# Last tiles that end with the last row, blank rows at fixed addresses, and outputs of the early tiles sent later

## What is computed

```python
h = layernorm(x) * (1 + ca) + sa
x = x + ga * attention(h)                      # per row
h = layernorm(x) * (1 + cb) + sb
gates = softmax((h @ w_red) @ wg_n.T);  idx = argmax(gates)      # one expert for each row
y = gelu(h @ w1[idx] + b1[idx]) @ w2[idx] + b2[idx]
x = x + gb * y * gates[idx]
```

## Time and profile before

| | |
|---|---|
| median of 3 runs | 321.43 us (321.24 to 325.39) |
| the profiled execution | 321.42 us |
| its span, first to last instruction | 319.7 us |
| mean granted TensorE clock | 0.949 of 2.4 GHz |
| busy: PE, DVE, ACT, POOL | 86%, 74%, 70%, 49% |

### The profile page before, as it was taken

One profiled execution on the slowest core, in us unless ns is written; L12 is line 12 of the kernel. 1 busy time (PEld: TensorE's weight loads), 2 busy tenths in 40 slices (PEclk: granted clock), 3 DMA queues, 4 the chain that ended last, 5 costly groups with the idle time before them and its releaser, 6 DMA issues. The chain is left out here.

```text
span 319.7 us, 11500 instructions
## 1 busy us (share of the span) xinstructions
PE 275.4 (86%) x4012; PEld 222.2 (70%) x4013; DVE 236.5 (74%) x769; ACT 224.2 (70%) x510; POOL 158.0 (49%) x173
## 2 busy tenths in 40 slices
PE   8789799999999999999999977684949699999960
PEld 3555577777777677687677756574849599999950
DVE  2767969989979989899899999595523456666740
ACT  1377788999889799889898689364237276676730
POOL 7104144362684774755746804557743434455550
PEclk9999999999999999999999999898578899999995
DMA  5996000000010011010100205134954424444400
GB/s 148 322 333 181 0 3 4 2 2 4 4 51 27 28 51 51 29 51 28 50 28 29 76 27 152 49 102 126 243 148 121 109 67 126 119 124 108 125 22 0
DMA packets 16240, 26.16 MB, mean 82 GB/s; under 512 B 2607, under 2 KB 11059, under 8 KB 16192
## 3 DMA queue, kind: packets, MB, share of 16 engines
q1 hardware_dynamic: 12464, 16.50, 18.8%
q0 software_dynamic: 3296, 8.41, 7.7%
q10 hardware_dynamic: 432, 0.59, 0.6%
HBM read 15.32 MB, written 10.64 MB: 81 GB/s over the span
## 5 line engine op out<-in xcount | busy, mean ns | idle before, releaser
L1129 DVE SCALAR_TENSOR_TENSOR phi<-ps,ebuf 128x512 f32<-128x512 f32 x128 | 82.0, 682 | 17.9 <-ACT ebuf L540 17.4
L536 ACT ACTIVATE ebuf<-ps 128x1024 f32<-128x1024 f32 x64 | 65.6, 1026 | 16.4 <-PE ps L766 15.6
L540 ACT ACTIVATE ebuf<-ebuf 128x512 f32<-128x512 f32 x128 | 74.4, 636 | 0.1
L764 PE MATMUL ps<-hT_hi,mix_lo 128*128 128x512 f32 x128 | 58.4, 456 | 8.2 <-DVE phi L1129 4.9
L594 ACT ACTIVATE gT<-ps,b_cols 128x128 f32<-128x128 f32 x156 | 44.7, 368 | 19.8 <-issue 13.6
L866 PE MATMUL ps<-w_sb,gT 128*128 x312 | 45.9, 294 | 13.2 <-DVE y L1446 11.3
L866 PEld LDWEIGHTS ps<-w_sb,gT 128*128 128x128 f32 x312 | 41.2, 206 | 15.2 <-issue 15.2
L766 PE MATMUL ps<-hT_hi,mix_hi 128*128 128x512 f32 x128 | 50.6, 396 | 0.0
L765 PE MATMUL ps<-hT_lo,mix_hi 128*128 128x512 f32 x128 | 50.6, 395 | 0.0
L495 POOL DMA_INDIRECT out<-yo,tok x27 | 27.4, 1014 | 29.7 <-issue 15.9
L446 POOL DMA_INDIRECT sorted_rows<-rec,pos x32 | 33.0, 1030 | 8.8 <-issue 5.4
(11 more groups left out here) (197 smaller groups left out, 452.5 us busy)
## 6 DMA issues: line engine op xcount, KB each, us to landing
rin<-sorted_rows SPq DMA_DIRECT2D x39, 192.5 KB
w1b<-in_L_ffn_w SPq DMA_DIRECT2D x1, 2048.0 KB, 14.2
sorted_rows<-pad_rec SPq DMA_DIRECT2D x6, 192.5 KB
sorted_rows<-pad_rec ACTq DMA_DIRECT2D x3, 192.5 KB
w1b<-in_L_ffn_b SPq DMA_DIRECT2D x1, 512.0 KB, 6.0
sorted_rows<-rec,pos POOLq DMA_INDIRECT x32
out<-yo,tok POOLq DMA_INDIRECT x27
wmod_sb<-in_L_wmod SPq DMA_DIRECT2D x1, 384.0 KB, 3.5
```

The lines of the kernel that those rows point to most:

```text
L536: nc.scalar.activation(ebuf[:, h % 2, :, :], x_ps[h % 2], ACT.Relu, scale=-1.0).then_inc(s_neg, 1)
L540: nc.scalar.activation(ebuf[:, h % 2, j, :], ebuf[:, h % 2, j, :], ACT.Exp, scale=-1.0).then_inc(s_exp, 1)
L764: mm(x_ps[h % 2][:, j, :], mix_lo[:, j, h, :], hi, start=True, stop=False)
L1129: v.scalar_tensor_tensor(out=phi[:, h % 4, j, :], in0=x_ps[h % 2][:, j, :], scalar=0.0, in1=ebuf[:, h % 2, j, :], op0=ALU.max, op1=ALU.add ...
```

## The change

The blank rows move from behind the last row of each expert to the head of its region: every region's first 128 rows are blank records, written by SP near the start of the program (nine writes, one of them the former `DUMMY`), and the records begin 128 rows further down (`region0` starts at 128). The last tile of an expert is taken as the 128 rows that end with the expert's last row. It overlaps the tile before it (or the blank head where the expert has few rows); the rows that were in the tile before get T added to their number, and are so not written twice. Slots behind the last tile get the last tile again, with all rows turned blank. For that the table has a second hop, a limit and a mask `blank`. The eight `pad_region` writes and `carry_i` go. On POOL, the 12 early outputs are no longer sent in one go: numbers 0 to 5 go out each when the slot six later is finished, numbers 6 to 11 after slots 15, 19, 23, 27, 31 and 35; POOL's loop over the late outputs is written out.

```diff
 sp.wait_ge(c_dve, 1)
-sp.dma_start(sorted_rows[DUMMY:DUMMY + P, :], pad_rec[:, :]).then_inc(s_tail, 16)
+for e in range(E + 1):
+    sp.dma_start(sorted_rows[e * REGION:e * REGION + P, :], pad_rec[:, :]).then_inc(s_tail, 16)
...
-for s in range(RING, RING + RING // 2):
+for s in range(RING, EARLY):
     reload_slot(s, s % RING)
 sp.wait_ge(s_table, 1)
-for e in range(PADS_SP):
-    pad_region(sp, e)
-for s in range(RING + RING // 2, EARLY):
-    reload_slot(s, s % RING)
-sp.wait_ge(s_table, 2)
...
-g_.iota(region0[:, :], [[REGION, E]], base=0, ...)
+g_.iota(region0[:, :], [[REGION, E]], base=P, ...)
+g_.iota(slot_next[:, :], [[1, LATE]], base=1, ...)
+g_.iota(row_no[:, :], [[0, 1]], base=0, channel_multiplier=1, ...)
+g_.memset(last_row[:, E:E + 1], float(DUMMY))
...
-def put_early(s):
-    wait_then(f_yd, s + 1)
+def put_early(s, behind=0):
+    wait_then(f_yd, s + 1 + behind)
...
-for s in range(EARLY):
-    put_early(s)
-with pool.Fori(EARLY, WHOLE - RING + 1, RING) as s:
-    for b in range(RING):
-        put(s + b, b)
-for s in range(WHOLE, SLOTS):
+for s in range(RING):
+    put_early(s, RING)
+for s in range(EARLY, SLOTS):
     put(s, s % RING)
+    if s % 4 == 3 and s // 4 - 3 < EARLY - RING:
+        put_early(s // 4 - 3 + RING)
...
 gelu(5, 1)
-act.wait_ge(s_table, 1)
-for e in range(PADS_SP, E):
-    pad_region(act, e)
...
-    v.tensor_copy(at, rin[:, b, 3 * D:R])
+    if early:
+        v.tensor_copy(at, rin[:, b, 3 * D:R])
+    else:
+        v.scalar_tensor_tensor(out=at, in0=blank[:, bass.ds(s - EARLY, 1)], scalar=float(T), in1=rin[:, b, 3 * D:R],
+                               op0=ALU.mult, op1=ALU.add)
...
-v.tensor_copy(carry_i[:, :], carry[:, :]).then_inc(s_table, 1)
...
+v.tensor_scalar(last_row[:, 0:E], carry[:, :], -float(P), None, ALU.add).then_inc(s_last, 1)
...
+v.tensor_scalar(limit[:, :], last_row[:, 0:1], row_no[:, :], None, ALU.add)
...
+v.tensor_tensor(skip[:, 1, :], last_row[:, 1:E + 1], last_row[:, 0:E], ALU.subtract).then_inc(s_tab, 1)
...
-v.tensor_tensor(hop[:, :, :], past[:, :, :], skip[:, :]..., ALU.mult).then_inc(s_tab, 1)
+for i in range(2):
+    last = v.tensor_tensor(hop[:, i, :, :], past[:, :, :], skip[:, i, :]..., ALU.mult)
...
-v.tensor_reduce(rowf[:, 0, :], hop[:, :, :], AX.X, ALU.add).then_inc(s_tab, 1)
+v.tensor_reduce(rowf[:, :, :], hop[:, :, :, :], AX.X, ALU.add).then_inc(s_tab, 1)
...
-v.tensor_scalar(row_i[:, EARLY:SLOTS], rowf[:, 1, :], float(DUMMY), None, ALU.min).then_inc(s_table, 1)
+v.scalar_tensor_tensor(out=row_i[:, EARLY:SLOTS], in0=rowf[:, 1, :], scalar=last_row[:, 0:1], in1=raw[:, :],
+                       op0=ALU.add, op1=ALU.min).then_inc(s_table, 1)
...
+v.scalar_tensor_tensor(out=blank[:, :], in0=rowf[:, 1, :], scalar=limit[:, :], in1=raw[:, :],
+                       op0=ALU.add, op1=ALU.is_lt).then_inc(s_blank, 1)
```

More of the change, by code:

```diff
@@ L50, in adaln_kernel @@
     RECS = 3
-    PADS_SP = E - 3
     RING = 6
@@ L190, in adaln_kernel @@
         lden = sb("lden", [P, TG, E])
-        skip = sb("skip", [P, E])
+        skip = sb("skip", [P, 2, E])
+        last_row = sb("last_row", [P, E + 1])
+        limit = sb("limit", [P, 1])
+        row_no = sb("row_no", [P, 1])
+        blank = sb("blank", [P, LATE])
         past = sb("past", [P, LATE, E])
-        hop = sb("hop", [P, LATE, E])
+        hop = sb("hop", [P, 2, LATE, E])
         expf = sb("expf", [P, LATE])
         rowf = sb("rowf", [P, 2, LATE])
+        raw = sb("raw", [P, LATE])
         region0 = sb("region0", [P, E])
@@ L198, in adaln_kernel @@
         slot_no = sb("slot_no", [P, SLOTS])
+        slot_next = sb("slot_next", [P, LATE])
         exp_i = sb("exp_i", [P, SLOTS], I32)
         row_i = sb("row_i", [P, SLOTS], I32)
-        carry_i = sb("carry_i", [P, E], I32)
         rin = sb("rin", [P, RING, R])
@@ L680, in _ @@
             gelu(EARLY - 1, (EARLY - 1) % 2)
-            act.wait_ge(s_table, 3)
+            act.wait_ge(s_table, 2)
             keep_in(EARLY, EARLY)
@@ L1295, in early_past @@
                 dve.wait_ge(s_ta, 6)
-                v.tensor_tensor(hop[:, 0:EARLY, :], past[:, 0:EARLY, :], skip[:, :].unsqueeze(1).broadcast_to([P, EARLY, E]), ALU.mult)
+                v.tensor_tensor(hop[:, 0, 0:EARLY, :], past[:, 0:EARLY, :], skip[:, 0, :].unsqueeze(1).broadcast_to([P, EARLY, E]), ALU.mult)
                 v.tensor_reduce(expf[:, 0:EARLY], past[:, 0:EARLY, :], AX.X, ALU.add).then_inc(s_ta, 1)
                 dve.wait_ge(s_ta, 7)
-                v.tensor_reduce(rowf[:, 0, 0:EARLY], hop[:, 0:EARLY, :], AX.X, ALU.add).then_inc(s_ta, 1)
+                v.tensor_reduce(rowf[:, 0, 0:EARLY], hop[:, 0, 0:EARLY, :], AX.X, ALU.add).then_inc(s_ta, 1)
             def early_table():
                 dve.wait_ge(s_ta, 8)
-                v.scalar_tensor_tensor(out=row_i[:, 0:EARLY], in0=slot_no[:, 0:EARLY], scalar=float(P), in1=rowf[:, 0, 0:EARLY],
+                v.scalar_tensor_tensor(out=row_i[:, 0:EARLY], in0=slot_next[:, 0:EARLY], scalar=float(P), in1=rowf[:, 0, 0:EARLY],
                                        op0=ALU.mult, op1=ALU.add).then_inc(s_early, 1)
@@ L1313, in early_rest @@
                 v.tensor_tensor(hop_a[:, :], done[:, 1:E + 1], done[:, 0:E], ALU.subtract).then_inc(s_ta, 1)
-                v.tensor_scalar(row_base[:, :], slot_no[:, 0:LATE], done[:, 0:1], float(P), ALU.add, ALU.mult)
+                v.tensor_scalar(row_base[:, :], slot_next[:, :], done[:, 0:1], float(P), ALU.add, ALU.mult)
                 dve.wait_ge(s_ta, 11)
@@ L1507, in _ @@
             v.tensor_tensor(upto[:, :, :], tri[:, :, :], rest[:, :].unsqueeze(1).broadcast_to([P, E, E]), ALU.mult)
-            v.scalar_tensor_tensor(out=skip[:, :], in0=rest[:, :], scalar=-float(P), in1=hop_a[:, :],
-                                   op0=ALU.mult, op1=ALU.add).then_inc(s_tab, 1)
+            v.scalar_tensor_tensor(out=skip[:, 0, :], in0=rest[:, :], scalar=-float(P), in1=hop_a[:, :],
+                                   op0=ALU.mult, op1=ALU.add)
+            v.tensor_tensor(skip[:, 1, :], last_row[:, 1:E + 1], last_row[:, 0:E], ALU.subtract).then_inc(s_tab, 1)
             dve.wait_ge(s_tab, 5)
@@ L1515, in _ @@
             dve.wait_ge(s_tab, 7)
[L1516 removed]
+            for i in range(2):
+                last = v.tensor_tensor(hop[:, i, :, :], past[:, :, :], skip[:, i, :].unsqueeze(1).broadcast_to([P, LATE, E]), ALU.mult)
+            last.then_inc(s_tab, 1)
             dve.wait_ge(s_tab, 8)
[L1518 removed]
+            v.tensor_reduce(rowf[:, :, :], hop[:, :, :, :], AX.X, ALU.add).then_inc(s_tab, 1)
             dve.wait_ge(s_tab, 9)
[L1520 removed]
+            v.tensor_tensor(raw[:, :], rowf[:, 0, :], row_base[:, :], ALU.add).then_inc(s_tab, 1)
             dve.wait_ge(s_tab, 10)
[L1522 removed]
+            v.scalar_tensor_tensor(out=row_i[:, EARLY:SLOTS], in0=rowf[:, 1, :], scalar=last_row[:, 0:1], in1=raw[:, :],
+                                   op0=ALU.add, op1=ALU.min).then_inc(s_table, 1)
             v.tensor_reduce(expf[:, :], past[:, :, :], AX.X, ALU.add).then_inc(s_tab, 1)
@@ L1533, in _ @@
                 finish(s, s % RING)
+            dve.wait_ge(s_blank, 1)
             def run(s, b):
```

16 lines of the change are left out of this document (8 added, 8 removed).

## The result

The changed kernel takes 326.24 us in the median of 19 runs (324.73 to 329.59), the kernel before 322.99 us in 19 runs beside it (321.01 to 325.39): a ratio of 1.0115, 95% interval [1.009, 1.014]. Every ratio in this document is formed from the executions in the faster of two states alone, while the medians are of all, so that it can be off the quotient of the medians by up to 0.7%. It was forecast at 316.2 us (313.3 to 321.3), and it is slower.

A forecast was written before the change was run, and what follows sets the result against it. PE was taken to bound the late slots, and a stall on three engines slots 5 to 8. 321.4 - 5.6 + 0.1 + 0.1 + 0.4 = 316.4 us, with the clock's luck 316.2; range 313.3 to 321.3.

The forecast's parts named there:

- Removed: the stall: Slots 5 to 8: the wait of DVE, ACT and SP goes, 5.6 us won (5.1 to 6.2), longer table included.
- the lucky-clock rival: After 232 us: all lower-clock spells of PE go, 6.2 us won and 1.5 to 2 more, about 314; chance 0.21.
- Table: DVE's early table ahead of `add_bias(4)`: gets 1.1 us longer (0.8 to 1.6).
- Added at the start: Eight more blank writes from SP from 24.34 us on, and POOL setup: zero, at most 0.5; 0.1 in the sum.
- Moved: the early outputs: Late stretch: six more POOL writes of 1.0 us fit into its idle time; cost 0.1 us.
- Changed in the late slots: DVE's row-number copy becomes an operation with the mask: 0.4 us taken, bounds 0 and 2.7.
- The stall moves into the late slots: Three POOL outputs in a row after slots 15, 19, 23, 27, 31, 35 stall there: 329 us; chance 0.07.
- The price of one place: Each of the six late places with three outputs costs 1.3 to 3 us, taken as 2.2.
- double buffering: Late slots: absorbs 5 of the 13 us that the six places would cost.
- The outputs were not it: Early stall comes from POOL's records of group 7 and stays, if shorter: 319 to 322.5, say 321; chance 0.15.
- DVE becomes the bound: Late slots: DVE's mask operation costs 0.1 us per slot, 318.5; inside the forecast's range, no chance of its own.

The follow-up runs named there:

- without the late six: Changed kernel with early outputs 6 to 11 taken out of POOL's late loop, their rows left out of the output: 314.26 us, ratio 0.9747 to the kernel before.
- the new order alone: Kernel before, blank rows and table as they were, with only POOL's new order of outputs: 331.24 us, ratio 1.0189.
- The run to nowhere: Changed kernel with all row numbers of the six late early outputs out of bounds, so POOL works but nothing is written: 327.42 us, ratio 1.0113.
- the version with other milestones: Changed kernel, all twelve early outputs ahead of slot 12's, spread by waits on finished slots 5, 5, 6, 7, 8, 9, 10, 10, then four later points: 319.18 us.
- the run with the old order: Changed kernel with its 12 early outputs in one go behind the records of group 7, blank rows as changed: 321.26 us, ratio 0.9964.
- the last version: Changed kernel, twelve early outputs ahead of slot 12's, a 128x784 POOL memset behind writes except where DVE copies weights or ends the table: 317.19 us, ratio 0.9816.

## Why the prediction was wrong

*Removed: the stall.* Right in kind and too small. The forecast was 5.6 won with the table's 1.1 inside; without the late six the early span shrinks by 6.8 (34.75 to 27.96), which is the value of the lucky-clock rival (6.2 and up): the granted clock was 0.97 over 232 to 242 us, though 0.70 over 245 to 248. I gave the stall to blank writes and outputs together, and that holds for the sum: of the 6.8 us, moving the blank rows alone gave 0.6 (with the table's 1.0 inside), the new order alone 3.5, and only both give all. What I had not seen is that they act in two ways. The outputs hold up news; late blank rows alone make PE wait for slot 9's tile. *Table:* slot 4 took 5.73 us for 4.75, 0.98 for the 1.1 forecast.

*Added at the start.* Zero, as put: `add_bias(0)` at 206.79 for 207.37.

*Moved: the early outputs.* This is the step that failed: "In the late stretch POOL is busy 20.42 of 42 us; six more at 1.0 fit. ... Zero, with a margin of only 0.12; I take 0.1." They do fit: POOL is busy 21.37 of 42 after, and the last output follows the last `add_bias` by 1.82 us as before (1.81). But the sum priced POOL's time and not that of the engines whose news the writes hold up. That measured 12.0 us in time (326.24 against 314.26), 10.9 in the late span, for a forecast of 0.1. The Trainium skill's rule (SBUF — State Buffer, the warning that DVE can hold up a DMA issued from GpSimd) let me weigh the wrong direction: it is about what DVE does to POOL's write, here 0.3 us at most, and nothing in it covers PE's news.

*Changed in the late slots.* Forecast 0.4, measured nothing: the late span without the six is 51.22 with the mask, 51.60 without.

*The rivals.* "The stall moves into the late slots" had 0.07, and is what happened: places and mechanism as written, and a size of 13 less 5 against 10.9 measured. Its 329 does not follow from that size: 316.4 and 8 are 324.4, with all 13 it is 329.4, and 326.24 was measured. So the chance of 0.07 for more than 327.9 stood on a wrong sum. The price of one place was right (2.2; slots 17 to 33 lost 1.8 to 2.3 each, the sixth place about 1); double buffering, for which I took off 5, absorbed next to nothing at the first five: ACT waits for its transpose from the same moment as DVE for its sums, and PE needs both. My reasons against it were bytes (64 KB for 192) and the DMA share (0.44). The run to nowhere shows that bytes play no part, and the share even fell, to 0.38. The row for it was in the earlier trace rows, a "remote" wait of 1.27 us with four records in a row and nothing else. I had written that POOL's back-to-back writes alone do some of the stall, and then did not let that into the sum. "The outputs were not it" is refuted: with the records alone there was no stall at slots 5 to 8. "DVE becomes the bound" is refuted by the 51.22.

## What stays open

What is shown is that POOL's own work on indirect writes that follow each other 1.3 us apart holds up the news, whatever they move, and that between writes 1.8 us and more apart it was never seen. What exactly starts a hold is not shown. Two writes can be enough: in the changed kernel two records start at 199.54 and 200.92, and ACT takes the transpose that PE finished at 200.22 only at 202.39, "remote"; every version has this place. A news item crossed four records unharmed at 229.14 in the changed kernel; in the version with other milestones ACT had PE's transpose at 236.01, 0.04 us after its end, with two close writes before it and a third just begun (233.39 to 236.96). Yet at 261.08 two close writes on top of the steady stream were enough. A backlog that builds up would fit some of these and not all. Runs of two in the late slots, with the stream's own pace kept, were not tried. Nor is it known which part on the way from PE to DVE and ACT is held. It can't be that way alone, since SP's own instructions slow down too (the last section).

## What to carry to other kernels

Count a POOL indirect write not by its 1 us of a half-idle engine but by who waits for other engines' news while writes follow closely: look at the distance of their starts, and keep them apart (here 1.8 us). A queue that already runs at its steady pace has no free slots, even at half its busy time; what is put into it is caught up later, close together. And where several engines wait for PE, "remote" or long after its end, and go on within 0.2 us of each other, look for what POOL was writing.

## What the hardware showed that was not expected

- Six indirect writes that write nothing cost as much as six that do (late span 63.29 against 62.10, without them 51.22).
- A run of POOL writes also stretches SP: three fetches take 6.87 us to issue in the run with the old order, 2.60 in the changed kernel and 3.51 without the six. It is not waiting for news that makes it long. The same instructions, in the view of SP's line with the old order and then without the six (shortest, median, longest in ns), show single ones of 0.70 us:

```profile
L293 SPq MOVE rin<-sorted_rows x3: 17/29/699, 230.1 to 237.3; - x3
L293 SPq MOVE rin<-sorted_rows x3: 29/29/29, 229.9 to 233.1; - x3
```

- A POOL `memset` beside a DVE copy of 128x640 made that copy take 1.64 and 1.75 us for 0.47 to 0.49, and one of 1.54 is left in the last version, at 251.68, where nobody waited for it. Beside POOL's writes alone a copy took at most 0.72 (changed kernel). The Trainium skill (SBUF — State Buffer, the section on SBUF's two separate sides) says that the two engines share a port pair under an exclusive lock; the trace agrees in kind: all three copies ended 0.35 us after the `memset` beside them did. They lost more than its 0.77 us (up to 1.2) because they had begun before it, beside one of POOL's writes; what held them until it began no row shows.
